# Decoder layer with cross attention and routed experts: the gate folded into the cross attention's products, its steps spread anew over a turn, two norms on GpSimd

## The reference

```python
x = layernorm(x + self_attention(x))            # 16 heads of 16, no mask, softmax over 1024 keys
# cross attention: 77 context rows for each sequence, one head of width 256
q = x @ Wq + bq;  k = ctx @ Wk + bk;  v = ctx @ Wv + bv
x = layernorm(x + softmax(q @ k.T / 16) @ v)
# experts: 8 of them, 256 -> 1024 -> 256, each token goes to its best two
gate = softmax(x @ gate_w + gate_b)
topv, topi = top_k(gate, 2);  topv /= topv.sum(-1)
y = sum over the two: topv * (relu(x @ w1[e] + b1[e]) @ w2[e] + b2[e])
x = layernorm(x + y)
```

## Time and profile before

| what | value |
|---|---|
| median of three runs | 1436.06 us |
| span of the profiled execution, first to last instruction | 1435.9 us (a time of its own is not given beside it) |
| PE busy | 1400.5 us, 98% |
| DVE busy | 1076.8 us, 75% |
| ACT busy | 863.0 us, 60% |
| POOL busy | 556.4 us, 39% |
| chain that ended last, by engine | PE 81%, DVE 8%, issue 4%, POOL 3% |
| mean granted TensorE clock | 0.996 |

### The profile page before, as it was taken

The page is one execution under the profiler, slowest core; times in us unless marked ns, Lnnn a source line. Parts: engine busy times, 40 slices in busy tenths (PEclk is TensorE's granted clock), DMA queues, the critical chain, the costliest instruction groups (busy, mean ns, idle before and its releaser), DMA issues.

```text
span 1435.9 us, 48815 instructions
## 1 busy us (share of the span) xinstructions
PE 1400.5 (98%) x18550; PEld 933.5 (65%) x18550; DVE 1076.8 (75%) x1963; ACT 863.0 (60%) x1973; POOL 556.4 (39%) x952
## 2 busy tenths in 40 slices
PE   9999999999999999999999999999999999999995
PEld 5445455544444444444444448889889999999994
DVE  6888888888888888888999955767555655555553
ACT  4688888877777777778877783333233333333331
POOL 2221211222222222531213413677775555555554
PEclk9999999999999999999999999999999999999998
DMA  6235555444434323432422342222332222222221
GB/s 210 63 106 171 165 162 168 131 110 126 117 105 142 86 64 89 118 85 68 137 81 69 102 147 92 72 86 87 121 101 81 75 75 75 75 74 70 77 75 48
DMA packets 108799, 147.39 MB, mean 103 GB/s; under 512 B 28027, under 2 KB 80570, under 8 KB 107546
## 3 DMA queue, kind: packets, MB, share of 16 engines
q1 hardware_dynamic: 94026, 104.92, 25.6%
q0 software_dynamic: 13968, 38.05, 8.0%
q10 hardware_dynamic: 576, 1.31, 0.3%
HBM read 81.17 MB, written 63.04 MB: 100 GB/s over the span
## 4 chain that ended last, share of the span: by engine, by line
PE 81%; DVE 8%; issue 4%; POOL 3%; ACT 1%; DMA 1%; DVEq 0%; POOLq 0%; ACTq 0%
PE pa L939 15%; PE pa L1187 14%; PE pb L939 13%; PE po L1115 13%; PE pb L1201 13%; PE px L939 6%; DVE neg L1476 3%; PE px L932 2%; PE pb L932 1%; ACT w_sb L1304 1%; PE po L1046 1%; PE po L932 1%; PE px L1021 1%; PE px L993 1%; DMA space<-y_parts,y_tags 1%
## 5 line engine op out<-in xcount | busy, mean ns | idle before, releaser
L1476 DVE TENSOR_REDUCE neg<-pa 128x1 f32<-128x1024 f32 x512 | 611.4, 1213 | 76.8 <-PE pa L939 69.3
L1304 ACT ACTIVATE w_sb<-pb 128x512 f32<-128x512 f32 x996 | 590.0, 598 | 105.2 <-PE pb L939 69.7
L939 PE MATMUL pb<-w_sb 99*32 99x512 bf16 x3984 | 392.1, 380 | 3.6 <-ACT w_sb L1304 2.0
L1420 ACT ACTIVATE space<-pa,b1T_sb 128x128 f32<-128x128 f32 x568 | 154.3, 383 | 322.7 <-PE pa L1187 320.2
L939 PE MATMUL pa<-w_sb 96*32 96x512 bf16 (+1 forms) x4208 | 323.1, 380 | 6.1 <-DVE neg L1476 6.1
L1115 PE MATMUL po<-w_sb,space 128*32 128x256 f32 x4000 | 304.6, 379 | 0.0
L1187 PE MATMUL pa<-xgT,attn_t 128*128 128x128 f32 x2272 | 269.3, 276 | 2.9 <-DVE attn_t L1814 2.9
L1187 PEld LDWEIGHTS pa<-xgT,attn_t 128*128 128x128 f32 x2272 | 265.7, 192 | 8.9 <-issue 5.6
L1201 PE MATMUL pb<-w_sb,space 128*128 x1136 | 260.4, 379 | 0.0
L1201 PEld LDWEIGHTS pb<-w_sb,space 128*128 128x128 f32 x1136 | 208.8, 190 | 25.1 <-issue 0.3
L1115 PEld LDWEIGHTS po<-w_sb,space 128*32 128x32 f32 x4000 | 124.3, 111 | 98.6
(11 more groups left out here) (242 smaller groups left out, 1234.1 us busy)
## 6 DMA issues: line engine op xcount, KB each, us to landing
y_parts<-attn_t SPq DMA_DIRECT2D x13, 896.0 KB, 4.9
w_sb<-w SPq DMA_DIRECT2D x17, 512.0 KB, 4.7
attention_out<-space SPq DMA_DIRECT2D x64, 128.0 KB
w_sb<-w SPq DMA_DIRECT2D x7, 1024.0 KB, 8.0
xg<-x_by_expert SPq DMA_DIRECT2D x54, 130.0 KB, 2.1
q_parts<-w_sb SPq DMA_DIRECT2D x48, 128.0 KB, 3.1
w_sb<-q_parts SPq DMA_DIRECT2D x64, 96.0 KB, 2.6
w_sb<-k_parts SPq DMA_DIRECT2D x64, 96.0 KB, 3.0
```

The lines of the kernel that those rows point to most:

```text
L939: mm = pe.matmul(out[at:end], lhsT[:, at:end], rhs, start=start, stop=stop, tile_position=(0, at))
L1304: act.activation(ex_of(n)[:, half * HALF:(half + 1) * HALF], score_bank(n, half), ACT.Exp, scale=SCALE).then_inc(e_done, 1)
L1420: ins = act.activation(hT[tile % 2][:, f, :], pH[tile % 2][:, f, :], ACT.Relu, bias=g.b1_sb[:, bass.ds(e * FT + f, 1)])
L1476: dve.tensor_reduce(neg[i % 2][:, t:t + 1], pa[n % 2][:, :], AX.X, ALU.max, negate=True).then_inc(max_done, 1)
```

## The change

1. **The gate is folded into the cross attention.** `gate_w` is centred (its column mean is taken off), so that the product with it does not see the mean of a row. The 8 gate columns ride with other products: `fold` gets 8 more columns (CG = 85), which give x1 times the centred gate beside the scores; `cv` gets 8 more (DG = 264), which give the values times the gate. `mix` adds both, and the logits are that sum times the reciprocal deviation of the second norm, plus the bias. `turn_2`, its copy on ACT (`copy_2`) and `gate` are gone. 
2. **The bias of the scores is added by DVE** (`add_bias`, 85 columns, from PSUM into SBUF, behind `score`), not by a product with ones. `cross_max` and `soft` now read SBUF.
3. **The steps of a turn are spread anew:** `proj` in step 1, values in step 2, `turn_1` in step 3, `score` in step 4, none in step 5 (where `add_bias`, `cross_max` and `soft` stand), `turn_p` in 6 and `cross` in 7.
4. **Both norms of a turn run on POOL** (`norm_1_pool`, `norm_2_pool`); in the expert stage they stay on DVE.
5. **In the expert stage** `proj(j + 1)` stands at the end of a tile, into the free half of `po`; `turn_1` and `score` come one chunk of `down` earlier; DVE adds and measures tile j ahead of mixing tile j-1.
6. **Setup:** products in quarters, with new small ones for the mean of the gate, the values' gate and the biases.

```diff
@@ waits of the one bank px
-            if s == 1 and before is not None:
-                return c_copied, before + 1
-            if s == 2 and j is not None:
-                if ranks_step(p) is not None:
-                    return route, routed(ranks_step(p), "rank")
-                return (logits_done, before + 1) if before is not None else (added, j + 1)
-            if s == 3 and b:
+            if s == 1 and j is not None:
+                return (route, routed(ranks_step(p), "rank")) if ranks_step(p) is not None else (added, j + 1)
+            if s == 2 and b:
                 return v_done, nth(b, p // TURN % TB)
-            if s >= 4 and j is not None:
-                return ((b_copied, j + 1), (soft_done, j + 1), (p_copied, j + 1), (mixed, j + 1))[s - 4]
+            if j is not None:
+                return {3: (b_copied, j + 1), 4: (biased, j + 1), 6: (p_copied, j + 1), 7: (mixed, j + 1)}.get(s)
@@ POOL
+                def norm_1_pool(j):
+                    t = j % 2
+                    pool.tensor_tensor(nmean_a[:, :], mv_a[:, t, 0:1], minus[:, 0:1], ALU.mult).then_inc(nmean_1_done, 1)
+                    pool.wait_ge(nmean_1_done, j + 1)
+                    pool.wait_ge(rstd_1_done, j + 1)
+                    pool.tensor_scalar(x1[:, j % XR], x1[:, j % XR], nmean_a[:, 0:1], rstd_a[:, t:t + 1], ALU.add, ALU.mult
+                                       ).then_inc(norm_1_done, 1)
...
+                    if s == 0 and before is not None:
+                        norm_2_pool(before)
...
-                    if s == 3 and j is not None:
+                    if s == 2 and j is not None:
                         spread_1(j)
+                        norm_1_pool(j)
@@ PE
                 def score(j):
                     pe.wait_ge(b_copied, j + 1)
                     b = j // TB
-                    cols = slice(b * C, b * C + C)
-                    out = px[:, 0:C]
                     product = quarters if j < MAIN_PROJ else whole
                     for k in range(KD):
-                        product(out, turned_b[:, k, :], fold[:, b, k, :], k == 0, False)
-                    product(out, g.ones[:, :], fold_b[:, cols], False, True).then_inc(scored, 1)
+                        mm = product(px[:, 0:CG], turned_b[:, k, :], fold[:, b, k, :], k == 0, k == KD - 1)
+                    mm.then_inc(scored, 1)
...
                     elif s == 1:
-                        turn_2(before)
-                    elif s == 2:
                         proj(j)
-                        if before is not None:
-                            gate(before)
                         if ranks_step(p) is not None:
                             ranks(ranks_step(p))
+                    elif s == 2:
+                        project_v(quarters, px, xs, turn % 4 * P).then_inc(v_made, 1)
                     elif s == 3:
-                        project_v(quarters, px, xs, turn % 4 * P).then_inc(v_made, 1)
+                        turn_1(j)
                     elif s == 4:
-                        turn_1(j)
-                    elif s == 5:
                         score(j)
...
@@ PE, an expert tile
-                    if MAIN_PROJ < j < NT:
-                        pe.wait_ge(mixed, j)
-                        proj(j)
...
                     if tile + 2 < FFN_TILES:
+                        if MAIN_PROJ < j < NT:
+                            pe.wait_ge(added, j + 1)
                         turn_x(tile + 2)
...
                     down(tile, CHUNKS[0], e)
-                    if MAIN_GATE <= j - 1 < NT:
-                        if j < NT:
-                            pe.wait_ge(added, j + 1)
+                    if MAIN_PROJ <= j < NT:
+                        pe.wait_ge(mixed, j)
...
-                        turn_2(j - 1)
+                        turn_1(j)
                     down(tile, CHUNKS[1], e)
...
                     if MAIN_PROJ <= j < NT:
-                        pe.wait_ge(c_copied, j)
-                        turn_1(j)
+                        score(j)
                     down(tile, CHUNKS[2], e)
-                    if MAIN_PROJ <= j < NT:
-                        score(j)
-                    if MAIN_GATE <= j - 1 < NT:
-                        gate(j - 1)
+                    if MAIN_PROJ < j + 1 < NT:
+                        pe.wait_ge(x_taken, tile + 3)
+                        proj(j + 1)
@@ DVE
+                def add_bias(j):
+                    dve.wait_ge(scored, j + 1)
+                    if j >= XR:
+                        dve.wait_ge(p_turned, j - XR + 1)
+                    dve.tensor_tensor(scores[:, j % XR, :], px[:, 0:CG], bias[:, j // TB, :], ALU.add).then_inc(biased, 1)
+
                 def cross_max(j):
-                    dve.wait_ge(scored, j + 1)
+                    dve.wait_ge(biased, j + 1)
...
+                    dve.tensor_reduce(cneg[:, t:t + 1], keys[:, j % XR, :], AX.X, ALU.max, negate=True).then_inc(cmax_done, 1)
...
+                    dve.scalar_tensor_tensor(lg[:, j % 2, :], raw, rstd_b[:, j % 2:j % 2 + 1], g.gate_b_sb[:, :], ALU.mult, ALU.add
+                                             ).then_inc(logits_done, 1)
...
                     if s == 5 and j is not None:
+                        add_bias(j)
                         cross_max(j)
@@ DVE, an expert tile
+                    if MAIN_PROJ < j < NT:
+                        add(j)
+                        measure_1(j)
                     if MAIN_PROJ <= j - 1 < NT:
                         cross_rec(j - 1)
                         mix(j - 1)
                         measure_2(j - 1)
...
+                    if MAIN_PROJ <= j < NT:
+                        add_bias(j)
+                        cross_max(j)
                     if MAIN_GATE <= j - 1 < NT:
...
```

More of the change, by code:

```diff
@@ L14 @@
 C = 77
-CP = 96
 H, HD = 16, 16
@@ L196, in ranks_step @@
         b, first = divmod(turn - DELAY - 1, TB)
-        return b - 1 if s == 2 and first == 0 and b >= 1 else None
+        return b - 1 if s == 1 and first == 0 and b >= 1 else None
     def feeds(p):
         turn, s = divmod(p, TURN)
-        return (0, 3).index(s) if turn == TURNS - 1 and s in (0, 3) else None
+        return (0, 2).index(s) if turn == TURNS - 1 and s in (0, 2) else None
     def in_pa(n):
@@ new lines, in stream @@
+        scores, keys = rows_1[:, :, D:D + CG], rows_1[:, :, DG:DG + C]
+        flat_pay = [sb(f"pay{i}", [P, TB * PAYLOAD + DG - PAYLOAD]) for i in range(2)]
+        pay = [room[:, 0:TB * PAYLOAD].rearrange("p (t w) -> p t w", w=PAYLOAD) for room in flat_pay]
+        spare_pay = flat_pay[(B - 1) % 2]
+        last_ex = [spaces[0][:, :], spaces[2][:, :], spare_pay[:, 0:S], spare_pay[:, S:2 * S]]
+        turned_b = sb("turned_B", [P, KD, P])
+        o_last = sb("o_last", [4 * PER, QC])
+        to_dims = cv[0:4 * PER, 0:2, :].rearrange("p b d -> p (b d)")[:, 0:4 * P].rearrange("p (j m) -> p j m", j=4)
@@ new lines, in cross_weights @@
+                    first, last = k == 0, k == KD - 1
+                    if i == MEAN:
+                        mm = quarters(bank[:, 0:NE], g.ones[:, :], g.gate_sb[:, k, :], first, last)
+                    elif i in KEYS:
+                        at = KEYS.index(i) * P
+                        mm = quarters(bank[:, 0:B * C], c_w[:, 0, k, at:at + P], c_x[:, k, :], first, last)
+                    elif i == VALUE_GATES:
+                        for m in range(KD):
+                            mm = quarters(bank[:, k * NE:(k + 1) * NE], c_wvT[:, m, k * P:(k + 1) * P], gate_c[:, m, :],
+                                          m == 0, m == KD - 1)
+                    elif i in VALUES:
+                        b = VALUES.index(i)
+                        mm = quarters(bank[0:C, 0:DG], c_x[:, k, b * C:(b + 1) * C], c_wv[:, k, :], first, last)
+                    elif i in FOLDS:
+                        at = FOLDS.index(i) * P
+                        mm = quarters(bank[:, 0:B * C], c_w[:, 1, k, at:at + P], c_k[:, k, :], first, last)
+                    elif i == BIAS:
+                        mm = quarters(bank[:, 0:B * C], bq_wide[:, k, :], c_k[:, k, :], first, last)
+                    else:
+                        mm = quarters(bank[:, 0:NE], bv_wide[:, k, :], gate_c[:, k, :], first, last)
@@ L1367, in behind @@
                         high_part(b, turn % TB)
-                    elif s == 1 and before is not None:
-                        copy_2(before)
-                    elif s == 3 and b:
+                    elif s == 2 and b:
                         i = turn % TB
@@ L1375, in behind @@
                         take_v(px, b, i, v_done)
-                    elif s == 4 and j is not None:
+                    elif s == 3 and j is not None:
                         copy_1(j)
@@ L1397, in _ @@
                 act.wait_ge(set_up, SET_UP)
-                for n in range(len(WEIGHTS)):
-                    take_weights(n)
+                for i in range(ITEMS):
+                    take_weights(i)
```

(13 more changed lines are left out.)

330 lines of the change are left out of this document (169 added, 161 removed).

## The result

| what | before | changed | forecast |
|---|---|---|---|
| median | 1435.8 us (4 runs) | 1443.2 us (4 runs, 1439.9 to 1445.7) | 1428.7 us |
| ratio of the runs, 95% interval | | 1.0049 [1.0038, 1.0061] | 0.995 |
| span of the profiled run | 1435.9 us | 1443.9 us | |
| mean granted clock | 0.996 | 0.991 | |

A forecast was written before the change was run, and what follows sets the result against it. PE, 98% busy, was taken as the bound, with delays of DVE's `cneg` paid by PE in full. Turns +1.1, turn 31 -0.7, setup -0.3 and experts -7.5 gave -7.4 us: 1428.7 us, own range 1424 to 1433.5, 8 in 10 1420 to 1437.

The forecast's parts named there:

- the rest of a turn: Turns 9 to 30, outside PE savings and step 6: moved projection and POOL norms covered, table or routing meetings +1 us.
- The five table and routing turns: Turns where DVE's table or routing step meets the projection's sum and statistics in step 1: +1 us (0 to +3).
- two pairs, over 5 us: Time POOL's root, negated mean and norm (1.5 to 2.2 us) have until `turn_1`; so they cost nothing.
- The growth of step 6: PE's stall behind `soft` grows from 0.22 to 0.89 us, by 0.67 in each of 22 turns: 14.7 us.
- Work off PE: Transposes, gate and product with ones leave PE in turns 9 to 30: net 0.69 us in 21 turns, sum 14.6 us.
- A plain turn: Token-tile turn stays as long as before: work taken off PE (-14.6 us) is handed back as waiting (+14.7 us).
- The two signs of being wrong: Prediction wrong if step 6 is under 3.3 us, or expert tiles with cross attention stay above 10.2 us.
- Rival A: Whole kernel: PE's work comes off whole, step 6 stall staying at 0.2 us; 1409.5 us, chance 0.12.
- The circle: Expert tiles with cross attention: a loop of DVE and POOL dependences sets 9.7 us, above PE's 9.4.
- nearly full there: Expert stage before the change: DVE and POOL have almost no idle time in a cross-attention tile of 10.63 us.
- Rival B: Expert tile: POOL's root comes later, circle 10.6 us instead of 9.7, eating the gain; slower, 1440 us, chance 0.14.

The follow-up runs named there:

- x1: The changed kernel with the old step order (projection a step later) in turns 9, 17 and 25 only: 1436.0 us, ratio to before 1.0001.
- x7: The changed kernel with both norms of a turn back on DVE, only the roots on POOL: 1446.9 us, ratio to before 1.0081.
- x2: The changed kernel with DVE's bias addition and maximum over the scores ahead of its first self-attention maximum of step 5: 1421.5 us, ratio to before 0.9896.
- x5: The changed kernel with x1, x2 (except turns 9, 17, 25), x4, the table in seven small steps and two scatters moved: 1412.3 us, ratio to before 0.9835.
- x4: The changed kernel with an expert tile's second norm behind both halves of copy_w1, not between them: 1440.8 us, ratio to before 1.0026.
- x8: x5 with POOL's scaling of the heads behind its norm in turns 13, 21 and 29: 1411.6 us, ratio to before 0.9828.
- x3: The changed kernel with the long table step in step 3 of turn 29, not step 1: 1441.2 us, ratio to before 1.0039.

## Why the prediction was wrong

**What failed.** One step of the part "the rest of a turn": "`proj` in step 1 with its sum and statistics on DVE: PE's next side job or the longer pair covers them." I costed the moved step by what it issues, and not by what it waits for. `proj` of a sequence's first tile reads heads that POOL scales only once the reciprocals have come back by DMA. In turn 25 of the kernel before, POOL and PE read:

```profile
693.33 2.36 POOL L768 TENSOR_TENSOR attn_t<-attn_t,space 128x1024 f32<-128x1024 f32 x1 [0.75 <-DMA space<-reciprocals]
...
696.81 1.04 PE L939 MATMUL px<-woT_sb,attn_t 128*32 128x256 f32 x16
```

`proj` had 1.1 us to spare (693.33 + 2.36 = 695.69), and the move takes a pair away, 2.9 us in this turn. These two make 1.9 of the 2.67 us of waiting (0.14 us go from the scaling's end to `proj`). The other 0.75 is the scaling itself, which starts 5.71 us after the start of the turn and not 4.96; why, no run separates. The forecast held nothing for this step. It cost 9.7 us in the profiled run, with the lower clock behind two of the waits, and x1 gives 7.1 us back by the medians. With 7.1 to 9.7 in the sum the forecast would have been 1435.8 to 1438.4, no change.

**What was mis-sized.** The five table and routing turns stood at +1 (0 to +3). Turn 29 alone is +3.8. The prediction had the 2.2 us of the earlier trace rows as the table's own time. But that instruction stood beside POOL's scaling, and in the changed kernel, where it comes behind it (L1709), it takes 0.37 us. Two rows of the kernel before and one of the changed:

```profile
796.49 2.38 POOL L768 TENSOR_TENSOR attn_t<-attn_t,space 128x1024 f32<-128x1024 f32 x1 [2.82 <-PE pb L939]
796.88 2.21 DVE L1663 TENSOR_TENSOR xg<-xg,tiles_e 128x200 f32<-128x200 f32 x1
...
809.94 0.37 DVE L1709 TENSOR_TENSOR xg<-xg,tiles_e 128x200 f32<-128x200 f32 x1
```

So the long instruction is whichever meets the scaling, here the table's first. And the prediction had no term for the clock: the waits in turns 9, 25 and 29 are followed by a stretch at 1.2 GHz, about 6 us in all. Turn 21 (+1.0) is POOL's queue: for root and norm I counted "two pairs, over 5 us", while the scaling, two scatters and the parts of the next sequence stand ahead of them there. x7 shows that the place of the norm itself does not matter to this wait, since the root stays on POOL.

**What held.** The growth of step 6: forecast 0.67, measured 0.74. By x1 it is 0.30 for the moved `score` and 0.13 for the product with ones, together 0.43 (forecast 0.40), and 0.31 for `add_bias` (forecast 0.27). Work off PE: forecast 0.69 a turn, measured 0.70 (0.48 in step 1, 0.12 in step 2, 0.10 in step 5). `soft` 1.69 us after the maximum, forecast 1.7. A plain turn costs +0.05, forecast about 0. The two signs of being wrong that the prediction named (step 6 under 3.3 us, tiles above 10.2 us) both stayed away, at 3.93 and 10.10 us: they watch the plain step and the tile, and the loss came in turns that they do not look at. Rival A (PE's work comes off whole, 1409.5) did not happen, but x2 shows how near it was: with two DVE instructions ahead of a maximum the stall of 0.93 us goes in all 22 turns, and with the waits of the odd turns gone too (x5) the time is 1412. The rule of the Trainium skill named in the prediction (Perfetto Trace Analysis, Identifying Performance Opportunities: a kernel generally improves by improving the most-contended engine) did not give the time of this change, which took 18 us of work off PE and lost 7 us. It comes near only once those waits are away.

**The experts.** The circle was 0.4 us short, for the wait on the second root; x4 gives 9.67 without it. Its reading that DVE and POOL are "nearly full there" was wrong: in the tile of the earlier trace rows they are busy for 7.8 of 10.63 us each. Rival B put the slowness here, and it was not here. Tiles 3 to 11 gave 7.1 us, near the forecast; 1.6 us were given back in tiles 14 to 17 (7.63 to 7.85 us, before 7.24 to 7.67). I did not find out why. My guess, not shown, is POOL's scatters of the last sequence, two in each of these tiles, for which PE had a lead before.

**What stays open.** Of x5 and x8 some 3 us are missing against the sum. Steps 5 and 7 of turn 28 are 0.3 to 0.5 us long in both. And the time of the changed kernel varies by 6 us (1439.9 to 1445.7), where x8's varies by 2.4. The wait of turn 25 moves with the landing of the DMA (its step 1 is 5.8 to 7.9 us in the profiles), which fits. So does the clock, which fell behind some waits and not behind others as long (below). No run separates them.

## What to carry to other kernels

When a step is moved ahead, look up what it waits for in its worst turn, not in the plain one: what the move takes beyond the margin between the releaser's end and the step's start (in the rows of that turn) is the least that it costs, and a plain turn that comes out right proves nothing about the others. When work comes off the busiest engine, ask which instruction of the next engine sits behind a long one that it does not need. Here moving two DVE instructions ahead of a 1.2 us maximum was worth 1.5% (21.6 us), more than all that was taken off PE (18 us).

## What the runs showed of the hardware

- **A DVE instruction can be held for all of a POOL instruction.** Beside POOL's 128x1024 product (2.4 us) one table product took 2.06 us and 0.35 apart from it (changed, x3), another 2.21 and 0.37 (before, changed), a norm 1.95 and 0.40 (x7), logits of 8 columns 1.88 and 0.22 (x8); each ended within 0.25 us of POOL's end. Not held, in turn 29 of the changed kernel, were the statistics at 806.74 us (0.43 us as elsewhere), which overlap the same instruction, and their aggregate at 807.35 us (0.18 us as elsewhere), which begins inside it. The Trainium skill (SBUF — State Buffer, Who interferes with whom) has the rule: an instruction of DVE with two inputs in SBUF, or in a mode that uses both of its ports, shares a port pair with GpSimd, and the one that comes later waits in full. These rows agree: the products and the logits have two inputs in SBUF, the statistics one; which mode the norm used no row shows. The prediction did not use it, though the earlier trace rows were a case of it.
- **The other way round:** POOL's root over one column took 1.07 us beside DVE's copy of w1 (0.84 to 1.09 over the tiles) and 0.57 apart.
- **Short waits can cost twice, and their length alone does not decide it.** Behind PE's idle times of 1.78, 2.67 and 3.09 us the granted clock was 0.5 for some us (windows above), which cost about 6 us beside the 7.5 us of the waits themselves. In x4 it fell behind 1.77 us in turn 9, too. But it stayed at 1.00 behind 1.76 us in turn 9 of x7, 2.19 us in turn 25 of x3 and 2.43 us in turn 25 of x4. What makes the difference is not shown.
